# Projection of a Fourier layer's modes: two weight terms combined on VectorE before a 128-column table

## The reference, cut to what matters

```python
x_ft = rfft2(xt) / scale_fwd
a = x_ft[:, :, :32, :32]                  # 32 x 32 complex modes a channel
blk1 = complex_matmul(a, fw1)             # a 64x64 complex weight for each mode
blk2 = complex_matmul(a, fw2)
out_ft[:, :, :32, :32] = blk1             # wave numbers 0 .. 31
out_ft[:, :, 224:, :32] = blk2            # wave numbers -32 .. -1
out = irfft2(out_ft) / scale_bwd
x = x + relu(out @ W + b + out)
```

## Time and profile before

| | |
|---|---|
| median of 3 runs | 2145.39 us (2144.99 to 2149.75) |
| the profiled execution | 2151.67 us, its span 2149.8 us |
| TensorE's mean granted clock | 0.928 |
| PE busy | 1885.0 us (88%) |
| PEld busy (weight loads, beside PE) | 1499.1 us (70%) |
| DVE busy | 1417.9 us (66%) |
| ACT busy | 1149.4 us (53%) |
| POOL busy | 273.4 us (13%) |
| mean DMA rate | 254 GB/s |
| the projection's passes L1066, PE | 512 in 126.4 us |

### The profile page before, as it was taken

One profiled execution on the slowest core, in us unless ns is written; L12 is line 12 of the kernel. 1 busy time (PEld: TensorE's weight loads), 2 busy tenths in 40 slices (PEclk: granted clock), 3 DMA queues, 4 the chain that ended last, 5 costly groups with the idle time before them and its releaser, 6 DMA issues.

```text
span 2149.8 us, 57900 instructions
## 1 busy us (share of the span) xinstructions
PE 1885.0 (88%) x24558; PEld 1499.1 (70%) x24558; DVE 1417.9 (66%) x2151; ACT 1149.4 (53%) x1881; POOL 273.4 (13%) x514
## 2 busy tenths in 40 slices
PE   5899998999639577888459999999999999999999
PEld 3677766777524566767447887878878778787887
DVE  5866776677144732222147887878878788887887
ACT  5755655556114312111146776666767667676665
POOL 0000000000000300000201404032040400404000
PEclk9999999999855589999769999999999999999999
DMA  8877887785396599999418878888788888879886
GB/s 310 310 246 242 275 265 227 249 270 197 75 141 79 124 246 267 255 253 269 147 39 285 285 305 320 306 317 295 276 316 305 320 292 273 306 294 332 313 298 250
DMA packets 210171, 546.86 MB, mean 254 GB/s; under 512 B 64322, under 2 KB 139586, under 8 KB 173634
## 3 DMA queue, kind: packets, MB, share of 16 engines
q1 hardware_dynamic: 150866, 458.18, 63.6%
q10 hardware_dynamic: 53680, 41.95, 7.8%
q0 software_dynamic: 5376, 43.07, 6.9%
HBM read 361.68 MB, written 148.96 MB: 238 GB/s over the span
## 4 chain that ended last, share of the span: by engine, by line
PE 41%; DMA 8%; DVE 1%; ACT 0%; POOL 0%; issue 0%; POOLq 0%; DVEq 0%
PE ps_y L1393 13%; PE ps_xt L1345 9%; PE ps_wave L1379 9%; DMA x_in<-in_x 7%; PE ps_col L1360 6%; PE ps_y L1383 4%; DMA planes_in<-planes 1%; DMA tile<-high_tile 0%; DVE by_channel L770 0%; DVE low_tile L1288 0%; ACT high_tile L1241 0%; POOL tile L1219 0%; POOL planes_in L1207 0%; DVE y_out L1317 0%; POOL low_tile L1219 0%
## 5 line engine op out<-in xcount | busy, mean ns | idle before, releaser
L1247 ACT ACTIVATE x_turned<-ps_xt 128x512 f16<-128x512 f32 x512 | 305.7, 597 | 325.0 <-PE ps_xt L1345 325.0
L1393 PE MATMUL ps_y<-apply,x_turned 128*128 128x128 f16 x6144 | 428.3, 220 | 0.0
L1393 PEld LDWEIGHTS ps_y<-apply,x_turned 128*128 128x128 f16 x6144 | 377.6, 98 | 64.5 <-issue 0.6
L1296 DVE TENSOR_TENSOR x_turned<-ps_xt,x_turned 128x512 f16<-128x512 f32 x512 | 351.4, 686 | 98.4 <-ACT x_turned L1247 98.3
L221 DVE TENSOR_TENSOR parts<-stage,parts 128x1024 f16<-128x1024 f32 x256 | 301.9, 1220 | 120.8 <-ACT parts L145 120.3
L1317 DVE SCALAR_TENSOR_TENSOR y_out<-ps_y,relu 128x512 f32<-128x512 f32 x512 | 351.2, 686 | 22.0 <-PE ps_y L1393 2.4
L1345 PE MATMUL ps_xt<-c_eye,x_in 128*128 128x128 f32 x2048 | 312.7, 276 | 13.6 <-DMA x_in<-in_x 13.6
L1257 ACT ACTIVATE relu<-ps_wave 128x512 f32<-128x512 f32 x512 | 303.3, 592 | 13.7 <-PE ps_wave L1379 13.6
L145 ACT ACTIVATE parts<-stage 128x1024 f16<-128x1024 f32 x256 | 255.1, 1049 | 77.6 <-issue 42.3
L290 PE MATMUL row_ps<-parts,c_rows_dft 128*64 128x512 f16 x1536 | 202.1, 391 | 62.0 <-DVE parts L221 53.7
L1288 DVE SCALAR_TENSOR_TENSOR low_tile<-ps_col,high_tile 128x512 f16<-128x512 f32 x256 | 176.8, 691 | 104.8 <-ACT high_tile L1241 104.8
(11 more groups left out here) (124 smaller groups left out, 1857.0 us busy)
## 6 DMA issues: line engine op xcount, KB each, us to landing
stage<-in_x SPq DMA_DIRECT2D x256, 512.0 KB, 4.8
x_in<-in_x SPq DMA_DIRECT2D x128, 1024.0 KB, 11.0
out_y<-y_out SPq DMA_DIRECT2D x128, 1024.0 KB, 6.9
fw_first<-in_fw SPq DMA_DIRECT2D x9, 2048.0 KB, 16.5
fw<-in_fw ACTq DMA_DIRECT2D x8, 2048.0 KB, 20.4
fw<-in_fw SPq DMA_DIRECT2D x8, 2048.0 KB, 18.5
fw_first<-in_fw ACTq DMA_DIRECT2D x7, 2048.0 KB, 20.1
tile<-high_tile POOLq DMA_DIRECT2D x48, 240.0 KB, 13.5
```

The source lines that it names most:

```text
L1247: nc.scalar.activation(turned[u % 2][:, 0, :, :], ps_turn[u % 2][:, :, :], ACT.Copy).then_inc(turn_high, 1)
L1296: nc.vector.tensor_tensor(v[:, 1, :, :], ps_turn[u % 2][:, :, :], v[:, 0, :, :], ALU.subtract).then_inc(turn_split, 1)
L1393: mm = nc.tensor.matmul(ps_y[u % 2][:, :, 2 * k:2 * k + 2], turned[u % 2][:, p, k, :], apply[:, bass.ds(b, 1), q, :, :].rearrange("p o c w ...
```

## The change

The table loses its index f: it holds, for each part r and each h (cosine or sine), one row of 128 columns. A new function `add(k)` on DVE makes two tensors of 128x512 float32 from the two terms in T: first + second (for the cosine rows) and first - second (for the sine rows). k = 32 gets a copy and a negated copy, k = 0 uses T itself. Two buffers `sums` hold them. `project(k)` then makes, for each half bh and each h, two products (r) of 128x128 by 128 columns instead of four of 256: eight products, again two passes each. The semaphore `sums_ready` takes the place of `turn_taken` ahead of a projection and of `out_ready` where ACT asks whether a T buffer is free. The order within a step changes on three engines: TensorE now does turn, mix, project; ACT take_turn, take_high, stores, load; DVE take_mixed, take_low, add for the next step's projections. Table set-up takes 8 instructions in place of 16.

```diff
+            def add(k):
+                if k == 0:
+                    return
+                n = sums_number(k)
+                for f in terms(k):
+                    dve.wait_ge(turn_taken, 2 * (slot_of(f, k) + 1))
+                if n >= 2:
+                    dve.wait_ge(out_ready, number[[j for j in order if j != 0][n - 2]] + 1)
+                second = turned(slot_of(1, k))[:, 1, :, :, :].rearrange("p r b y -> p (r b y)")
+                to = sums[n % 2][:, :, :, :, :].rearrange("p s r b y -> p s (r b y)")
+                if k == K1:
+                    nc.vector.tensor_copy(to[:, 0, :], second)
+                    nc.vector.tensor_scalar(to[:, 1, :], second, -1.0, None, ALU.mult).then_inc(sums_ready, 1)
+                else:
+                    first = turned(slot_of(0, k))[:, 0, :, :, :].rearrange("p r b y -> p (r b y)")
+                    nc.vector.tensor_tensor(to[:, 0, :], first, second, ALU.add)
+                    nc.vector.tensor_tensor(to[:, 1, :], first, second, ALU.subtract).then_inc(sums_ready, 1)
...
@@ DVE's steps
             for step in range(STEPS + 8):
+                if step < STEPS:
+                    take_mixed(step)
                 for k in project_at(step):
                     take_low(k)
-                if step < STEPS:
-                    take_mixed(step)
+                for k in project_at(step + 1):
+                    add(k)
...
@@ project(k)
-                for f in terms(k):
-                    pe.wait_ge(turn_taken, 2 * (slot_of(f, k) + 1))
+                if k == 0:
+                    pe.wait_ge(turn_taken, 2 * (slot_of(0, 0) + 1))
+                else:
+                    pe.wait_ge(sums_ready, sums_number(k) + 1)
...
                 for bh in range(2):
-                    pairs = [(f, r) for f in terms(k) for r in range(2)]
-                    for f, r in pairs:
...
+                    for h in range(2):
+                        for r in range(2):
+                            v = turned(slot_of(0, 0))[:, 0] if k == 0 else sums[sums_number(k) % 2][:, h]
+                            last = nc.tensor.matmul(
+                                ps_out[n % 2][:, bh, :, h, :], v[:, r, bh * HB:(bh + 1) * HB, :].rearrange("p b y -> p (b y)"),
+                                table[:, r, h, :, :], start=(r == 0),
+                                stop=(r == 1 and (k, h) != (0, 0)))
...
@@ TensorE's steps
             for step in range(STEPS + 8):
-                for k in project_at(step):
-                    project(k)
                 slot = turn_at(step)
                 if slot is not None:
                     turn(slot)
                 if step < STEPS:
                     mix(step)
+                for k in project_at(step):
+                    project(k)
```

More of the change, by code:

```diff
@@ L837, in mix_project @@
         out = [m.sb(f"project_out{i}", [P, 2, 2, 2, 2, FLUSH, C], F16) for i in range(2)]
-        table = m.sb("project_table", [P, 2, 2, 2, 2, C])
+        sums = [m.sb(f"mix_sums{i}", [P, 2, 2, B, K1]) for i in range(2)]
+        table = m.sb("project_table", [P, 2, 2, 2, C])
         W_eye = m.sb("W_eye", [P, C])
@@ L861, in mix_project, with sums_number @@
         block = m.stack.enter_context(nc.Block())
+        def sums_number(k):
+            return number[k] - (number[0] < number[k])
         def turned(slot):
@@ L932, in take_turn @@
                         before = slot - KC if slot % KC else slot - 2 * KC
+                        if before == 0:
+                            act.wait_ge(out_ready, number[0] + 1)
                         if before >= 0:
-                            act.wait_ge(out_ready, max(number[k] for k in range(K1 + 1) for f in terms(k)
-                                                       if slot_of(f, k) == before) + 1)
+                            act.wait_ge(sums_ready, max(sums_number(k) for k in range(1, K1 + 1) for f in terms(k)
+                                                        if slot_of(f, k) == before) + 1)
                     y0 = i * MG // 2
@@ L953, in _ @@
             for step in range(STEPS + 8):
+                slot = turn_at(step)
+                if slot is not None:
+                    take_turn(slot)
                 for k in project_at(step):
@@ L957, in _ @@
                     store(act, blk, 1, stored_sin)
-                slot = turn_at(step)
-                if slot is not None:
-                    take_turn(slot)
                 if step % KC == KC - 1 and step // KC + SL < LOADS:
@@ L1000, in _ @@
                 nc.vector.tensor_tensor(W_eye[half, :], w["W"][half, :], w["eye"][half, half], ALU.add).then_inc(table_cleared, 1)
-            nc.vector.memset(table[:, :, :, :, :, :], 0.0).then_inc(table_cleared, 1)
+            nc.vector.memset(table[:, :, :, :, :], 0.0).then_inc(table_cleared, 1)
             nc.vector.memset(first_y[:, :], 0.0).then_inc(table_cleared, 1)
             dve.wait_ge(table_cleared, 4)
-            for f in range(2):
-                for r in range(2):
-                    for part in range(2):
-                        for h in range(2):
-                            half, g = slice(part * C, (part + 1) * C), (r + part + h) % 2
-                            minus = (r, part) == (1, 1) if h == 0 else ((r, part) == (0, 0)) != (f == 1)
-                            nc.vector.tensor_scalar(table[half, f, r, g, h, :], W_eye[half, :], -1.0 if minus else 1.0, None,
-                                                    ALU.mult).then_inc(table_ready, 1)
+            for r in range(2):
+                for part in range(2):
+                    for h in range(2):
+                        half, g = slice(part * C, (part + 1) * C), (r + part + h) % 2
+                        minus = (r, part) == (1, 1) if h == 0 else (r, part) == (0, 0)
+                        nc.vector.tensor_scalar(table[half, r, h, g, :], W_eye[half, :], -1.0 if minus else 1.0, None,
+                                                ALU.mult).then_inc(table_ready, 1)
             nc.vector.memset(first_y[:, 0::K1], 1.0).then_inc(table_ready, 1)
@@ L1063, in project @@
                 for bh in range(2):
-                    pairs = [(f, r) for f in terms(k) for r in range(2)]
-                    for f, r in pairs:
-                        last = nc.tensor.matmul(
-                            ps_out[n % 2][:, bh, :, :, :].rearrange("p g h c -> p (g h c)"),
-                            turned(slot_of(f, k))[:, f, r, bh * HB:(bh + 1) * HB, :].rearrange("p b y -> p (b y)"),
-                            table[:, f, r, :, :, :].rearrange("p g h c -> p (g h c)"), start=((f, r) == pairs[0]),
-                            stop=((f, r) == pairs[-1] and k > 0))
-                    if k == 0:
-                        last = nc.tensor.matmul(ps_out[n % 2][:, bh, 0, 0, :], first_y[0:1, :], bias_n[0:1, :],
-                                                start=False, stop=True)
+                    for h in range(2):
+                        for r in range(2):
+                            v = turned(slot_of(0, 0))[:, 0] if k == 0 else sums[sums_number(k) % 2][:, h]
[3 more added lines that the diff above has]
+                                stop=(r == 1 and (k, h) != (0, 0)))
+                        if (k, h) == (0, 0):
+                            last = nc.tensor.matmul(ps_out[n % 2][:, bh, 0, 0, :], first_y[0:1, :], bias_n[0:1, :],
+                                                    start=False, stop=True)
                 last.then_inc(out_ready, 1)
             for step in range(STEPS + 8):
-                for k in project_at(step):
-                    project(k)
                 slot = turn_at(step)
```

3 lines of the change are left out of this document (2 added, 1 removed).

## The result

The changed kernel takes 2162.21 us (median of 6 runs, 2159.01 to 2167.31), the kernel before 2146.63 us in the 6 runs beside it (2144.99 to 2149.75). The ratio is 1.0075, with an interval of 1.0055 to 1.0095: 15.6 us slower between the medians. The steps of the forecast are less right than its sum, as the traces show, so a part of the hit is luck.

What follows compares the result with a forecast made beforehand. No engine was full; the even-load buffer's own loop, landing time plus landing to next issue, set the pace. Terms +1, +10.6 and -1 gave +10.6 us, so 2145.39 became 2156, range 2138 to 2180.

Steps and rivals of the forecast that it cites:

- The ring: Even loads: each projection waits for the previous one's passes, ACT's copy, DVE's low part and sums; 4.75 us, TensorE idle 1.7.
- The pass of 128 columns: TensorE's projection: 0.112 us a pass, 2.0 us to the end of 16, against 3.72 us for 256 columns.
- Rival D: Projection passes don't halve, taking 2.7 us for 16: +19 us, 2175; chance 0.07.
- TensorE's saving: Projections of 31 k each take 1.85 us less, so TensorE's time falls by 57 us.
- From landing to the last mix: Even loads' steps after landing grow from 12.2 to 13.8 us, 1.6 more; landing to issue with stores, 2.9 more.
- The first loads: Even loads 2 and 4: TensorE is the pace, next issue 2.4 us sooner, then returned by load 4: +1 in all.
- The tail: Last odd load's steps and four more projections: 28.1 us in place of 29.1, 1 less.
- Rival C: TensorE stays at the lower clock through even loads' work after waits: 43 us more, 2199; chance 0.08.
- the stores' issue: In loads 4, 8 and 12 four stores take 3.3 us of each queue, with the next load behind them.
- The stretch: Even landings take 21.6 and 24.3 us, not 17.6, because the odd load is issued into them; its earlier issue costed at nothing.
- Rival A: Even loads land undisturbed in 17.6 us, as the skill's rule of queues served in turn implies: 2119 us; chance 0.12.
- The per-load terms of the forecast: Stage: +1 for loads 2 and 4, +10.6 for loads 6 to 14, -1 for the tail: +10.6 us.

Runs made afterwards that it cites:

- run 1: The changed kernel with two VectorE loops swapped, so the sums come before the low part: 2143.04 us against 2145.87 for the kernel before, ratio 0.9986.
- run 8: The changed kernel with one of VectorE's two sums left out, sine rows using the other: 2153.47 us against 2144.14 for the kernel before, ratio 1.0047.
- run 3: The kernel before with 128-column passes, old order, no sums, half the sum left out: 2133.38 us against 2145.87, ratio 0.9937.
- Run 7: The kernel before, with SP's half of each odd load held back until the even load landed: 2174.54 us against 2144.14, ratio 1.0100.
- run 5: The changed kernel with the four stores issued a step later, behind the next load: 2154.87 us against 2144.14 for the kernel before, ratio 1.0045.
- run 6: The changed kernel with the edits of run 4 and run 5 together: 2158.93 us against 2144.14 for the kernel before, ratio 1.0062.
- run 4: The changed kernel with the old order on TensorE and ScalarE, sums ahead of VectorE's mix copy: 2134.93 us against 2145.87 for the kernel before, ratio 0.9947.

## Why the prediction was right, and where its steps were off

**The ring (right).** The forecast put the decision into one place: in even loads a projection waits for the whole way round, 4.75 us, with 1.7 of it idle. Measured are 4.67 and 1.40, and runs 1 and 8 show by taking links out that the time hangs on it. Its links were right but for the sums. They were costed at 0.677 us each and last 0.68 to 0.69, yet the second begins 0.60 behind the first (903.08, 903.68). The pair adds 1.20 to the ring, not 1.36. The Trainium skill ("VectorE: DVE Perf Modes", the section on the TRN2 errata) gives 691 ns for such an operation of 512 float32. The trace agrees with that as a duration; for the ring it is the distance between starts that counts.

**The pass of 128 columns (right).** 2.05 us for 16, forecast 2.0. Rival D needed 2.7 (its two parts, 0.06 and 0.107 us, stand in no row). But TensorE's saving was put at 57 us and is 45: behind waits the passes run slower (2.91 at 898.90, 3.78 at 1054.94).

**From landing to the last mix (mis-sized).** Forecast 12.2 to 13.8, +1.6. For loads 6 to 14 the traces give 13.4 to 14.0 before and 15.3 to 16.2 after, on average 13.8 and 15.8: +2.0. Both ends were 1.5 to 2 us too low, since what runs first behind a landing runs longer: a mix of 1.94 us in both kernels, and a projection of 2.91 in the kernel after. With stores, load 8 goes from landing to issue in 19.1 us (897.03 to 916.11) where it was 16.0 (895.56 to 911.54): +3.1, forecast +2.9.

By loads, from one even issue to the next:

| | forecast, us | measured, us |
|---|---|---|
| loads 2 and 4 | +1 | +6.1 |
| load 6 | +1.6 | +2.2 |
| load 8 | +2.9 | +1.4 |
| load 10 | +1.6 | +2.9 |
| load 12 | +2.9 | +6.5 |
| load 14 and the tail | +0.6 | +3.6 |

**The first loads (wrong).** The forecast let TensorE be the pace there and gave load 2 an issue 2.4 us sooner. It came 2.5 later: the even load 2 has a gap of 2.93 us without a releaser before a mix at 788.27, the projection behind it takes 3.20 us, and the third projection waits 1.39 us for its sums. In load 4 the ring stands whole, with 1.39 us of waiting before two projections, and the stores behind it: from its first mix to the next issue go 19.0 us in place of 14.8. I had treated the first loads as free of waits. What makes the gaps without a releaser isn't shown by any run here. They aren't the change's own (12.7 us in the stage, 15.7 before), but run 3 has 33.9.

**The tail (wrong in sign).** Forecast 28.1 us, 1 less than before. From the end of the last even mix (1036.9) to the last low part (1068.1) it took 31.2. The windows view of the tail, kernel after:

```profile
core 0: us, PE busy (x) PEld busy (x) DVE busy (x) ACT busy (x) POOL busy (x), PEclk, DMA share, GB/s
1048.00:1068.00 20.00, 12.55 (x87) 11.50 (x80) 7.59 (x13) 3.47 (x6) 0.00 (x0) 0.74 0.04 13
```

And its timeline:

```profile
1050.28 2.05 PE L1097 MATMUL project_ps<-project_table,mix_sums 128*128 128x128 f32 x16
...
1054.94 3.78 PE L1097 MATMUL project_ps<-project_table,mix_sums 128*128 128x128 f32 x16 [2.61 <-DVE mix_sums L999]
...
1061.34 5.36 PE L1097 MATMUL project_ps<-project_table,mix_sums 128*128 128x128 f32 x32 [2.61 <-DVE mix_sums L999]
```

With no mix to put in between, TensorE waits 2.61 us for each ring, and after the first such wait the same 16 passes take 3.78 us in place of 2.05, with the granted clock at 0.74 of full speed on average, so partly at 1.2 GHz. From 1030 to 1050 us the kernel before shows 1.00. The Trainium skill ("TensorE: Matmul & The Clock Gate", HAM oscillation) describes bursts that begin cold behind waits for a DMA; here the wait before it was one for DVE. Rival C, which I had for the even loads, happened in the tail, and cost about 3 us, not 43. At the head of each even load's work it happened too, as the windows view of the kernel after shows:

```profile
896.00:900.00 4.00, 2.97 (x69) 2.80 (x70) 0.69 (x1) 0.00 (x0) 0.00 (x0) 0.50 1.09 326
```

TensorE is granted 0.50 of full speed, 1.2 GHz, for these 4 us behind a wait of 6.67 us for the load. This burst, behind a wait for a DMA, does begin at the lower clock. The kernel before pays nearly the same (0.64 in the earlier trace rows), so little of it counts as a cost of the change.

**ACT's queue (not foreseen).** I costed the stores' issue and the next load as a delay of that load alone. ACT's own list has the turn's copy behind them:

```profile
912.58 4.36 ACTq L895 DMA_DIRECT2D planes<-project_out  x4
...
916.99 1.25 ACTq L878 DMA_DIRECT2D fw_first<-in_fw  x1
918.34 1.08 ACT L945 ACTIVATE mix_turned<-mix_turn_ps 128x512 f32<-128x512 f32 x2 [6.57 <-issue]
919.08 1.07 PE L1079 MATMUL mix_turn_ps<-c_eye,mixed 128*128 128x128 f32 x8 [2.55 <-ACT mix_turned L945]
```

The copy is held for 6.57 us by ACT's own issues, and TensorE's next turn waits 2.55 us for it. Such waits occur behind each of the three groups of stores, 5.8 us of TensorE in all. It lies in the odd load, which has slack, so only a part can have reached the end.

**The stretch (mis-sized).** That landings of 21 to 24 us come from the other buffer's issue was argued from three rows. The load of 983.29, the slowest of them, stood behind stores, and that of 949.19, with another load issued 14.1 us into it, landed after 19.2. Over all kernels the other load's issue adds 1.2 us on average, whenever it comes, and stores ahead 3.4 more (the table in 7). So the earlier odd issue of the changed kernel cost nothing that shows, as the sum had it, and landings of about 20 us and 22.5 to 25 behind stores were a sound number to reckon with. Rival A's 17.6 us didn't come: the even loads of the kernel after landed after 18.9 us or more. The rule of the Trainium skill that was weighed there ("DMA: Bandwidth & Descriptors", Queues, rings and completion order) was taken to mean that a load issued later can't hold the earlier one up. Run 7 speaks neither way, and the 20.0 us against 18.8 speak against that reading, though weakly.

**The balance.** The per-load terms of the forecast gave +10.6, the stage shows +22.7 in the profiled execution, more than twice that, and the medians +15.6. Of those 12 us more in the stage, 5 lie in loads 2 and 4, 3.6 in load 12 (1.9 of it a landing after 21.3 us in place of 19.4, which is within the spread of landings), and 3 in the tail with load 14. Between the two profiled executions 22.7 became 12 us of span, as the stage started 5.2 us sooner and what follows it took 5.8 less; neither comes from the change as far as a run shows. Had the whole of 22.7 reached the medians, the forecast would have been 13 us low and not 6, still inside its range. That is the part that was luck.

## What to carry to other kernels

When work moves from the full engine to a free one, look first at where the new operation stands in that engine's list: two sums of 1.2 us behind a copy that waits for the very projection cost 18 us, and ahead of it nothing that could be told from noise. Before believing a saving on the busiest engine, take it out by itself with the rest unchanged: here halving 126 us of passes was worth 12.5, and most of the rest came back as waits for loads and as gaps. Count each DMA issue on an engine that also computes as work in its list, and keep it away from the moment after a large load.

## What the runs showed of the hardware that was not expected

- The issue of four stores takes 3.2 to 3.6 us (once 4.36, ACT in the kernel after) when the queue holds no new load, and 9 to 10.3 us on SP (9.83 and, in run 5, 9.28, 8.99 and 10.34) or 12.7 to 13.9 us on ACT (runs 5 and 6) right behind the issue of a 2 MB load. ACT computes nothing in that time. In the kernel after, ACT's issue of an odd load that comes 8.6 us behind an even one takes 4.62 us (846.31) in place of 0.6.
- TensorE's gaps without a releaser grew from 15.7 to 33.9 us in the stage when its passes were halved with everything else the same (run 3). In the kernels that also had the sums they were 12.7 (after), 19.1 (run 1) and 23.2 (run 4).
- Two float32 sums of 512 elements a partition begin 0.60 us apart on VectorE though each lasts 0.68.
- An even load of 2 x 2 MB lands 17.9 to 20.0 us after its issue when the next load comes 18 us behind or later, 19.0 to 21.5 when it comes 11 to 18 us behind, no matter when, and 21.1 to 25.4 behind 2 x 4 stores. Stores issued right behind it don't delay it (17.9 to 19.2 in runs 5 and 6).
- In the tail the passes behind a wait of 2.61 us ran at 3.78 us for 16 in place of 2.05, and the mean granted clock of those 20 us was 0.74, though no DMA was waited for.
